# Two-batch attention and mixture-of-experts kernel: another order of the query groups (0 1 2 3 5 6 7 4), groups 0 and 4 in halves, keys of two groups loaded by heads where the batch changes

## The chip, the core and the metric

The kernel runs on one core of a Trainium2 chip. The metric is the device time of one execution in microseconds (us); the lower the better. TensorE is called PE in the rows, VectorE DVE, ScalarE ACT, GpSimd POOL, and the engine that issues all DMAs SP.

## What is computed

The input is x of shape (2, 2048, 256): two batches of 2048 tokens, that is 16 tiles of 128 tokens per batch, 32 tiles in all. Two blocks follow each other, and a layer norm stands behind each.

```python
x = layernorm(x + local_attention(x))          # windows of 128 queries, 256 keys
x = layernorm(x + ffn_block(x))

def ffn_block(x):                              # 16 heads of width 16, causal over 2048 keys
    q_in = k_in = rope(x)
    scores = einsum('bqhd,bkhd->bhqk', q, k) / sqrt(16)
    attn = softmax(where(causal, scores, -inf))
    attn_out = (attn @ v) @ out_proj_w.T + out_proj_b
    x1 = layer_norm(x + attn_out)
    gates = softmax(x1 @ gate_w.T + gate_b)    # 8 experts, the 2 best are kept
    moe_out = sum over the 2 best of gate * (x1 @ expert_w[e].T + expert_b[e])
    return layer_norm(x1 + moe_out)
```

## The kernel before

The work is cut into steps, and each step belongs to one engine.

**Early stage of a tile** (steps whose names begin with a and r, one set per tile of 128 tokens): the local attention, its layer norm, the rotary embedding, the projections to q, k and v, and the split of q and k into three bf16 parts, which are stored to DRAM. Key parts are loaded into `ks` (steps kst), query parts into `qs` (steps qst).

**Attention of a query group**: four tiles are one group of 512 queries. Groups 0 to 3 are batch 0, groups 4 to 7 batch 1. Group s of a batch sees the keys of the groups up to itself in the batch, so groups 3 and 7 see 16 key tiles, and groups 0 and 4 see 4. A group is worked off in jobs of four heads each. A job has three parts. First `mx`: scores with queries as rows (L1373, with a mask at L1377), whose row maxima VectorE takes (L1065). The negated maxima are split, transposed (L1382) and stored as three more rows of `qs` (L806). Then `st`: scores with keys as rows, with the maxima subtracted by those three rows (L1401, mask L1406), and ScalarE's exponential into `pbuf` (L978). Then `pv`: after each four key tiles one run of products with v (L1424, 32 instructions of the hardware). `mx` of the next job is interleaved with `st` of the present one. At a job's end ScalarE empties the sum (osb), PE transposes it (L1430), VectorE divides (L1109, L1119).

**Late stage of a tile** (steps d, f, g): transposition of the context (L1506), output projection (L1513), layer norm on VectorE and GpSimd (to L1210, which writes x1), transposition of x1 (L1518), gate product (L1523), the choice of two experts on VectorE (L1218 to L1274), transposition of the weights (L1527), bias product (L1532), four expert blocks f_e0 to f_e3 (L1537), sums on VectorE, ScalarE and GpSimd, two layer norms on VectorE (L1304 to L1334), the store. A tile's late stage needs all four heads' jobs of its tiles. Its buffers exist once for the tiles at places 0 to 28 in the order (`late_set` gives 0), so those go through it one behind another: the transposition of x1 of a tile waits for block f_e3 of the tile before (`("f_e3", l)`, and VectorE's g_y L1304 of the one before stands in front of parts of the next one's gate). Places 29, 30 and 31 have buffers of their own.

**Order.** `ORDER` lists the groups; a group in `HALVED` is worked off in two halves of two tiles, so in eight jobs instead of four. `plan()` puts all steps of all engines into one list: a greedy pass that takes the step that can begin first by the durations written in the code, and of those that begin together the one with the lowest rank. The rank of an early step is its tile number less 5 and some (`turn`). Each engine executes its steps in that order, whatever the chip's real times are. Group 4 (`s == GB`) is the first of batch 1; its keys go into the part of `ks` that group 0's keys held. They are loaded by heads (steps kh, L768): the keys for heads 0 to 3 once the last group of batch 0 is through with these heads, and so on; all other keys of batch 1 wait for the end of batch 0.

```python
ORDER = (0, 1, 2, 3, 4, 5, 6, 7)
HALVED = (0, 7)
LATE = [GT * s + u for s in ORDER for u in range(GT)]
add("d_x1T", T, "PE", 215, ("d_aff", T), ("f_e3", l))
add("f_acc0", T, "DVE", 330, ("f_b", T), ("d_aff", T), ("g_aff2", l))
add("f_wT", T, "PE", 100, ("f_ws", T), ("f_b", l), ("f_es", l))
```

Of the kernel before, what the change touches and what calls it, by code (L numbers as in the profile page):

```python
# [22 lines left out]
GT = 4  # L23
# [3 lines left out]
HJ = 4  # L27
# [20 lines left out]

ORDER = (0, 1, 2, 3, 4, 5, 6, 7)
HALVED = (0, 7)  # L50
LATE = [GT * s + u for s in ORDER for u in range(GT)]
JOBS = [(s, hg, j0, GT // (1 + (s in HALVED))) for s in ORDER for j0 in ((0, GT // 2) if s in HALVED else (0,))
        for hg in range(H // HJ)]
NJ = len(JOBS)


# [75 lines left out]
def pair_count(pair):  # L132

    return sum(1 for x in range(pair % 4, pair + 1, 4) if x * 2 // GT != GB)

# [57 lines left out]
def stage_steps():  # L193
# [3 lines left out]
    def add(name, T, engine, ns, *before):  # L197
        turn = {"a": -1.0, "d": 5.0, "f": 6.0, "g": 7.0, "w": -2.0}.get(name[0], 0.0) - (name[:4] == "load")
        if name[0] not in "dfg":
            turn -= 5  # L200
        rows[name, T] = engine, ns, T + turn + sum(x[0][0] == name[0] and x[1] == T for x in rows) / 32, \
            [x for x in before if x[1] >= 0]
# [19 lines left out]
    for T in range(NT):  # L222
# [36 lines left out]
        for k in range(3):  # L259
            s, L = T // GT, LATE.index(T)  # L260
            if s == GB:

                for hg in range(H // HJ):
                    add(f"kh{hg}{k}", T, "SP", 400, ("pst", T), ("pv_end", last_job(GB - 1) - H // HJ + 1 + hg))
            else:
                add(f"kst{k}", T, "SP", 400, ("pst", T), *[("ones_later", 0)] * (T >= LEAD),
                    *[("pv_end", last_job(GB - 1))] * (s > GB))
            add(f"qst{k}", L, "SP", 400, ("pst", T), *[("pv_end", last_job(L // GT - 2))] * (L >= 2 * GT))

    for T in range(NT):  # L270
# [35 lines left out]
        add("f_acc0", T, "DVE", 330, ("f_b", T), ("d_aff", T), ("g_aff2", l))  # L306
        add("f_e0", T, "PE", 1720, ("d_x1Tc", T))
        add("f_e0c", T, "DVE", 860, ("f_e0", T), ("f_acc0", T), ("f_wts", T))
# [26 lines left out]
def job_steps():  # L335
# [8 lines left out]
    for J in range(NJ):  # L344
# [6 lines left out]
        for i, (c, j, h, heads, cols) in enumerate(mx_list(J)):  # L351
            diag = c == s % GB
            rows["mx", J, i] = ("PE", heads * max(cols / 2.4 + 3, 98) + (220 if cols == P else 95 * heads) * diag, r + length * i / n,
                                [(f"kh{hg}{k}" if s == GB else f"kst{k}", newest) for k in range(3)] +
                                [(f"qst{k}", LATE.index(newest)) for k in range(3)])
            rows["mr", J, i] = ("DVE", heads * cols / 0.96 + 55, r + length * i / n,
                                [("mx", J, i)] + ([("nm_a", J - 1)] if J else []))
# [106 lines left out]
def build(nc, windows, cs, w_qk_t, w_out, in_t, in_b, wo_t, gate_t, exp_t, exp_b, rows, gate_b, out):  # L464
# [6 lines left out]
    with ExitStack() as ctx:  # L471
# [204 lines left out]
        def _(sp):  # L676
# [3 lines left out]
            for step in order:  # L680
# [67 lines left out]
                elif name[:3] == "kst":  # L748
                    s, pair = T // GT, T // 2
                    _, slot, n, a = STACKS[3 + int(name[3:])]  # L750
                    sp.wait_ge(parts_stored[e], 16 * early_count(T))
                    if s > GB:

# [7 lines left out]
                elif name[:2] == "kh":  # L761
# [5 lines left out]
                    r0 = T * (NPART * 2 * E) + (NPART + a) * E  # L767
                    sp.dma_start(ks5[slot * DH:(slot + n) * DH, GB % KRING, T % GT, hg * HJ:(hg + 1) * HJ],  # L768
                                 parts_dram[r0:r0 + n * E, :].rearrange("(d h) t -> d h t", h=H)[:, hg * HJ:(hg + 1) * HJ])\
# [568 lines left out]
        def _(pe):  # L1338
# [3 lines left out]
            for step in order:  # L1342
# [7 lines left out]
                if name == "mx":  # L1350
# [5 lines left out]
                    if i == 0 and hg == 0:  # L1356

                        for pair in range(k_known, (GT * s + j0 + nj) // 2):
                            if s != GB:
                                pe.wait_ge(k_loaded[pair % 4], PAIR * pair_count(pair))  # L1360
                        k_known = max(k_known, (GT * s + j0 + nj) // 2)
                        for pair in range((GT * pos + j0) // 2, (GT * pos + j0 + nj) // 2):
                            pe.wait_ge(q_loaded[pair % 4], PAIR * (pair // 4 + 1))
                    if i == 0 and s == GB:
                        pe.wait_ge(kh_loaded[hg], GT * 3 * 16)
                    kslot = ((s // GB) * GB + c) % KRING
# [222 lines left out]
```

## Time and profile before

| | |
|---|---|
| median of 3 runs | 1450.21 us (1449.8 to 1451.3) |
| the profiled execution's own time | 1447.28 us |
| its span, first to last instruction | 1445.5 us |
| PE busy | 1384.9 us, 96% |
| DVE busy | 1089.6 us, 75% |
| ACT busy | 783.6 us, 54% |
| POOL busy | 428.0 us, 30% |
| mean granted clock of PE | 0.993 of full speed |

Busy time is the union of an engine's instructions. A stretch less the PE time in it is what PE stood idle there. A busy PE counts the time in which a matmul is still under way while the next has begun, so a stretch with no idle time can still be slower than the matmuls alone would allow.

### The profile page before, as it was taken

The numbers are of one execution on the slowest core, as the hardware profiler recorded it, in microseconds if no ns is written. First come the engines' busy times: TensorE is split into PE (matmuls) and PEld (weight loads), VectorE is DVE, ScalarE is ACT, GpSimd is POOL, SyncE is SP. The second block draws the span as 40 slices with busy tenths as digits, with TensorE's granted clock in tenths as the row PEclk, the third lists the DMA queues.
The fourth block names the chain that finished last, engine by engine and source line by source line (L and its number), as shares of the span: only waits on it lengthen the run. The fifth ranks groups of instructions, "written<-read, shape, count | busy, mean of one in ns | idle before, by whom it ended". The sixth has DMA issues, their size and how long they took to land.

```text
span 1445.5 us, 28119 instructions
## 1 busy us (share of the span) xinstructions
PE 1384.9 (96%) x9600; PEld 773.2 (53%) x9600; DVE 1089.6 (75%) x2736; ACT 783.6 (54%) x1707; POOL 428.0 (30%) x707
## 2 busy tenths in 40 slices
PE   7899999999999999999999999999999999999995
PEld 6767655554455445354656655555443355555542
DVE  3765877887787887778655897888778787888745
ACT  3235365555665555666655445554656467665651
POOL 4434522322232231122343543333121110111233
PEclk9999999999999999999999999999999999999997
DMA  3865422230211121120116232222120011111100
GB/s 116 201 172 128 124 57 61 58 85 21 63 46 46 38 62 33 40 57 20 50 49 156 79 90 68 57 57 65 29 60 21 22 24 29 33 32 33 34 23 12
DMA packets 152560, 88.57 MB, mean 61 GB/s; under 512 B 114430, under 2 KB 145974, under 8 KB 152163
## 3 DMA queue, kind: packets, MB, share of 16 engines
q1 hardware_dynamic: 152419, 86.78, 23.2%
q8 instruction: 78, 1.28, 0.4%
q14 instruction: 63, 0.52, 0.1%
HBM read 60.71 MB, written 25.43 MB: 60 GB/s over the span
## 4 chain that ended last, share of the span: by engine, by line
PE 44%; DVE 4%; ACT 3%; issue 2%; SPq 2%; DMA 2%; POOL 1%; POOLq 0%; DVEq 0%; ACTq 0%
PE bank L1537 11%; PE bank L1424 10%; PE bank L1401 8%; PE bank L1373 7%; ACT pbuf L978 2%; DVE mxs L1065 2%; SPq L806 1%; DMA qs<-nmT 1%; PE bank L1494 1%; PE bank L1377 1%; PE bank L1406 1%; PE bank L1513 1%; PE bank L1472 1%; PE bank L1480 1%; PE bank L1523 1%
## 5 line engine op out<-in xcount | busy, mean ns | idle before, releaser
L1065 DVE TENSOR_REDUCE mxs<-bank 128x1 f32<-128x512 f32 (+3 forms) x1120 | 709.4, 667 | 150.1 <-PE bank L1373 79.6
L978 ACT ACTIVATE pbuf<-bank 128x512 f32<-128x512 f32 (+1 forms) x1112 | 588.6, 599 | 326.1 <-PE bank L1401 151.0
L1401 PE MATMUL bank<-qs,ks 99*128 99x256 bf16 (+3 forms) x1536 | 420.7, 319 | 16.4 <-DMA qs<-nmT 10.9
L1373 PE MATMUL bank<-ks,qs 96*128 96x512 bf16 (+3 forms) x1280 | 423.0, 349 | 4.9 <-DVE mxs L1065 2.5
L1424 PE MATMUL bank<-pbuf,vcur 128*17 128x256 f32 (+3 forms) x3072 | 253.5, 469 | 0.3
L1401 PEld LDWEIGHTS bank<-qs,ks 99*128 99x128 bf16 x1536 | 142.3, 98 | 172.1 <-issue 56.3
L1537 PE MATMUL bank<-ew,x1T 128*128 128x512 f32 x464 | 222.4, 601 | 0.4 <-DVE mxs L1065 0.3
L1373 PEld LDWEIGHTS bank<-ks,qs 96*128 96x128 bf16 x1280 | 123.3, 98 | 129.7 <-issue 40.6
L1424 PEld LDWEIGHTS bank<-pbuf,vcur 128*17 128x17 f32 x3072 | 79.8, 97 | 147.4 <-issue 109.6
L1537 PEld LDWEIGHTS bank<-ew,x1T 128*128 128x128 f32 x464 | 82.0, 190 | 72.3 <-issue 60.8
L958 ACT ACTIVATE etmp<-bank,small 128x256 f32<-128x256 f32 x116 | 48.7, 471 | 80.1 <-PE bank L1537 80.1
L1377 PE MATMUL bank<-maskb,idb 128*128 128x128 bf16 x384 | 81.4, 220 | 0.0
L927 POOL TENSOR_TENSOR accp<-accp,etmp 128x256 f32<-128x256 f32 x29 | 21.1, 727 | 201.1 <-ACT etmp L958 201.1
L923 POOL TENSOR_TENSOR accp<-etmp 128x256 f32<-128x256 f32 x29 | 21.1, 728 | 188.6 <-ACT etmp L958 188.6
L1406 PE MATMUL bank<-idb,maskb 128*128 128x128 bf16 x352 | 73.6, 220 | 0.0
L1296 DVE SCALAR_TENSOR_TENSOR acc<-bank,small,acc 128x256 f32<-128x256 f32 x58 | 27.9, 480 | 52.7 <-PE bank L1537 52.7
L1494 PE MATMUL bank<-rxT,inw 128*128 128x128 f32 x464 | 57.0, 276 | 0.0
L1494 PEld LDWEIGHTS bank<-rxT,inw 128*128 128x128 f32 x464 | 55.1, 192 | 2.2 <-issue 1.3
L899 POOL CAST parts<-qkf 128x512 bf16<-128x512 f32 x28 | 17.4, 623 | 122.9 <-DVE qkf L1159 122.9
L873 POOL TENSOR_SCALAR small<-small 128x1 f32<-128x1 f32 x32 | 7.1, 223 | 156.5 <-DVE small L1143 156.3
L1377 PEld LDWEIGHTS bank<-maskb,idb 128*128 128x128 bf16 x384 | 37.8, 98 | 13.7 <-issue 8.9
L958 ACT ACTIVATE osb<-bank 128x512 f32<-128x512 f32 (+1 forms) x40 | 20.5, 512 | 43.7 <-PE bank L1424 43.1
(279 smaller groups left out, 1746.2 us busy)
## 6 DMA issues: line engine op xcount, KB each, us to landing
vcur<-v_scratch SPq DMA_DIRECT2D x92, 136.0 KB, 2.3
parts_scratch<-parts SPq DMA_DIRECT2D x29, 384.0 KB, 3.3
xw<-windows SPq DMA_DIRECT2D x29, 256.0 KB, 2.8
qs<-parts_scratch SPq DMA_DIRECT2D x32, 192.0 KB, 3.3
ks<-parts_scratch SPq DMA_DIRECT2D x28, 192.0 KB, 3.4
qs<-parts_scratch SPq DMA_DIRECT2D x32, 128.0 KB, 3.1
v_scratch<-vst SPq DMA_DIRECT2D x29, 136.0 KB, 2.4
x_scratch<-x SPq DMA_DIRECT2D x29, 128.0 KB, 1.7
```

What stands on the lines that cost most here:

```text
L923: pool.tensor_tensor(accp[f], etmp[f][:, 0, :], etmp[f][:, 1, :], ALU.add).then_inc(accp1_ready, 1)
L958: return nc.scalar.activation(o, i, ACT.Copy, scale=scale)
L978: nc.scalar.activation(pbuf[:, u0:u0 + heads, nj * P - cols:nj * P], bk[:, 0:heads * cols].rearrange("p (h t) -> p h t", h=heads), ACT.Exp)\
L1065: v.reduce_max(mxs[:, j * HJ + h:j * HJ + h + heads, c], bk[:, 0:heads * cols].rearrange("p (h t) -> p h t", h=heads), AX_X)\
L1296: v.scalar_tensor_tensor(out=acc[f], in0=bk[:, 0:E], scalar=wts[f][:, 2 * k:2 * k + 1], in1=acc[f], op0=ALU.mult, op1=ALU.add).then_inc(ha ...
L1373: last = mm(bk[:, x * cols:(x + 1) * cols].rearrange("p (n t) -> p n t", t=P), qs5[0:KR, pos % QRING, j, head, :], ks5[0:KR, kslot, 0:cols ...
L1377: last = mm(bk[:, x * cols + j * P:x * cols + (j + 1) * P], idb[:, :], maskb[:, :], start=False, stop=True)
L1401: last = mm(bk[:, x * cols:(x + 1) * cols].rearrange("p (n t) -> p n t", t=P), ks5[0:KR + NPART, kslot, kb % GT, head, :], qs5[0:KR + NPAR ...
L1406: last = mm(bk[:, x * cols:x * cols + P], maskb[:, :], idb[:, :], start=False, stop=True)
L1424: last = mm(obank[32 * h:32 * h + DV, r0:r1], vcur[:, kb, h, :], pbuf[:, (u0 + h) % PB, r0:r1], start=kb == 0, stop=kb == nk - 1, tile_pos ...
L1494: last = mm(bk[:, co * P:(co + 1) * P], inw[:, ci, co * P:(co + 1) * P], rxT[e][:, ci, :], start=ci == 0, stop=ci == EC - 1)
L1537: last = mm(bk[:, :], x1T[f][:, c, :], ew[:, c, k * 2 * E:(k + 1) * 2 * E], start=c == 0, stop=c == EC - 1)
```

## The change

The order of the groups becomes 0 1 2 3 5 6 7 4. Group 7 is no longer worked off in halves, group 4 is, and it comes last. Group 5 now follows batch 0, so the keys of groups 4 and 5 (8 tiles) are loaded by heads. The ranks of early steps of tiles 16 to 31 become lower, so that they come earlier. Step f_e0 of a tile now also comes behind f_b of the tile before.

```diff
-ORDER = (0, 1, 2, 3, 4, 5, 6, 7)
-HALVED = (0, 7)
+ORDER = (0, 1, 2, 3, 5, 6, 7, 4)
+HALVED = (0, 4)
+AT_CHANGE = range(GB, ORDER[GB] + 1)
...
-    return sum(1 for x in range(pair % 4, pair + 1, 4) if x * 2 // GT != GB)
+    return sum(1 for x in range(pair % 4, pair + 1, 4) if x * 2 // GT not in AT_CHANGE)
...
         if name[0] not in "dfg":
-            turn -= 5
+            turn += -5 if T < 16 else -7 - (T - 16) / 4 if T < 24 else -9
...
-            if s == GB:
+            if s in AT_CHANGE:
                 for hg in range(H // HJ):
                     add(f"kh{hg}{k}", T, "SP", 400, ("pst", T), ("pv_end", last_job(GB - 1) - H // HJ + 1 + hg))
...
-        add("f_e0", T, "PE", 1720, ("d_x1Tc", T))
+        add("f_e0", T, "PE", 1720, ("d_x1Tc", T), ("f_b", T - 1))
...
-                    if i == 0 and s == GB:
-                        pe.wait_ge(kh_loaded[hg], GT * 3 * 16)
+                    if i == 0 and pos == GB:
+                        pe.wait_ge(kh_loaded[hg], len(AT_CHANGE) * GT * 3 * 16)
```

Line numbers of the changed kernel are one higher in these parts of the code. Nothing moves on PE before the first job of group 2 is half through. Behind that, these are places where the order differs.

PE in a job of group 7, around one run of products with v, first of before. `ks,qs` are `mx` scores, `qs,ks` are `st` scores, `pbuf,vcur` is the run.

```order
L1373 MATMUL bank<-ks,qs 128x512
L1401 MATMUL bank<-qs,ks 128x256 x2
L1373 MATMUL bank<-ks,qs 128x512
L1401 MATMUL bank<-qs,ks 128x256 x2
L1523 MATMUL bank<-gw,x1T 128x8 x2
L1424 MATMUL bank<-pbuf,vcur 17x256 x16
L1401 MATMUL bank<-qs,ks 128x256 x2
L1373 MATMUL bank<-ks,qs 128x512
L1401 MATMUL bank<-qs,ks 128x256 x2
L1373 MATMUL bank<-ks,qs 128x512
```

The same place in the changed kernel:

```order
L1374 MATMUL bank<-ks,qs 128x512
L1402 MATMUL bank<-qs,ks 128x512
L1374 MATMUL bank<-ks,qs 128x512
L1402 MATMUL bank<-qs,ks 128x512
L1538 MATMUL bank<-ew,x1T 128x512 x2
L1425 MATMUL bank<-pbuf,vcur 17x512 x16
L1374 MATMUL bank<-ks,qs 128x512
L1402 MATMUL bank<-qs,ks 128x512
L1374 MATMUL bank<-ks,qs 128x512
L1402 MATMUL bank<-qs,ks 128x512
L1374 MATMUL bank<-ks,qs 128x512
L1402 MATMUL bank<-qs,ks 128x512
```

What moved: the `st` scores come as one of 512 columns instead of two of 256, and the run of 16 products is 512 columns wide instead of 256.

PE at the end of the program, first of before: from the last run of products with v to the transposition of x1 of place 31.

```order
L1424 MATMUL bank<-pbuf,vcur 17x256 x12
L1424 MATMUL bank<-pbuf,vcur 17x128 x4
L1537 MATMUL bank<-ew,xT 128x512 x2
L1430 MATMUL bank<-idf,osb 128x128 x2
L1537 MATMUL bank<-ew,xT 128x512 x2
L1506 MATMUL bank<-idf,ctxn 128x128 x4
L1513 MATMUL bank<-wo,qs 128x256 x4
L1518 MATMUL bank<-idf,qs 128x128 x2
L1523 MATMUL bank<-gw,qs 128x8 x2
L1537 MATMUL bank<-ew,qs 128x512 x2
L1518 MATMUL bank<-idf,qs 128x128 x2
L1523 MATMUL bank<-gw,qs 128x8 x2
```

The changed kernel, behind its last run of products with v, in which tiles 26 to 31 (by place) are still in their late stage:

```order
L1519 MATMUL bank<-idf,x 128x128 x2
L1507 MATMUL bank<-idf,ctxn 128x128 x2
L1524 MATMUL bank<-gw,x1T 128x8 x2
L1538 MATMUL bank<-ew,x1T 128x512 x2
L1514 MATMUL bank<-wo,qs 128x256 x4
L1528 MATMUL bank<-idb,wpad 128x128
L1533 MATMUL bank<-ebp,accp 128x256
L1538 MATMUL bank<-ew,x1T 128x512 x6
L1519 MATMUL bank<-idf,x 128x128 x4
L1519 MATMUL bank<-idf,qs 128x128 x2
L1524 MATMUL bank<-gw,x1T 128x8 x2
L1538 MATMUL bank<-ew,x1T 128x512 x2
```

What moved: before, two expert blocks of the tile at place 29 and the whole late stage of places 30 and 31 stood behind the last run. Now three blocks of place 26 and most of the late stage of places 27 to 31 stand there, and of these 27 and 28 share one set of buffers with 26. The rows above begin with the transposition of x1 of place 27 and end with the gate product and the first block of place 28.

VectorE in the gate of a late tile near the end, from the gate's logits (L1218) on. First of before (tile at place 28):

```order
L1218 TENSOR_TENSOR small<-bank,gb_sb 128x8
L1304 TENSOR_TENSOR acc<-acc,etmp 128x256
L1221 TENSOR_REDUCE small<-small 128x1
L1307 BN_STATS small<-acc 128x6
L1312 BN_AGGR small<-small 128x2
L1224 RECIPROCAL small<-small 128x1
L1315 SCALAR_TENSOR_TENSOR acc<-acc,small,rowv 128x256
L1227 TENSOR_SCALAR small<-small 128x8
L1232 MAX small<-small 128x8
L1321 SCALAR_TENSOR_TENSOR x0f<-acc,small,x0f 128x256
L1235 MAX_INDEX ix<-small 128x8
L1325 BN_STATS small<-x0f 128x6
```

The changed kernel, in the gate of the tile at place 27, a few rows behind its first (L1219):

```order
L1233 MAX small<-small 128x8
L1316 SCALAR_TENSOR_TENSOR acc<-acc,small,rowv 128x256
L1236 MAX_INDEX ix<-small 128x8
L1189 TENSOR_TENSOR qs<-bank,qs 128x256
L1241 CAST small<-ix 128x8
L1322 SCALAR_TENSOR_TENSOR x0f<-acc,small,x0f 128x256
L1247 SCALAR_TENSOR_TENSOR small<-small 128x8 x2
L1192 BN_STATS small<-qs 128x6
L1326 BN_STATS small<-x0f 128x6
L1253 TENSOR_TENSOR small<-small 128x8
L1197 BN_AGGR small<-small 128x2
L1189 TENSOR_TENSOR qs<-bank,qs 128x256
```

What moved: between the same instructions of the gate now stand, besides those of the last layer norms of the tile before (L1316, L1322, L1326, L1331), those of the first layer norm of tiles 30 and 31 (L1189, L1192, L1197). From the logits to the padded weights (L1274, now L1275) it was 24 instructions, a row with x2 counted twice, and is 28 for the tile at place 27 and 33 for that at place 28.

## Rows read from the trace of the kernel before

**Rows 1.** The page: busy time of each engine, share of the span, instructions.

```profile
PE 1384.9 (96%) x9600; PEld 773.2 (53%) x9600; DVE 1089.6 (75%) x2736; ACT 783.6 (54%) x1707; POOL 428.0 (30%) x707
```

**Rows 2.** Windows: stretch, its length, busy time (instructions) of each engine, PE clock, DMA.

```profile
400.00:448.10 48.10, 47.14 (x308) 24.96 (x307) 37.76 (x91) 27.92 (x61) 13.97 (x22) 1.00 0.14 38
...
683.00:756.50 73.50, 72.09 (x486) 43.68 (x486) 44.41 (x126) 43.44 (x98) 28.26 (x45) 1.00 0.17 47
756.50:839.60 83.10, 80.84 (x565) 50.98 (x564) 58.22 (x176) 40.41 (x95) 36.84 (x61) 1.00 0.40 107
839.60:1043.10 203.50, 200.75 (x1313) 111.54 (x1310) 163.99 (x413) 109.35 (x242) 68.22 (x111) 1.00 0.24 64
...
1088.10:1133.00 44.90, 42.50 (x260) 17.16 (x258) 34.42 (x85) 26.36 (x57) 6.42 (x11) 1.00 0.08 20
1133.00:1178.90 45.90, 43.52 (x256) 17.97 (x256) 40.83 (x115) 26.09 (x56) 8.19 (x15) 1.00 0.09 24
1178.90:1268.70 89.80, 89.37 (x890) 50.01 (x888) 69.09 (x153) 62.18 (x127) 8.72 (x15) 1.00 0.13 30
1268.70:1361.90 93.20, 91.90 (x781) 50.27 (x779) 79.80 (x193) 57.42 (x121) 16.18 (x28) 1.00 0.14 34
1361.90:1400.90 39.00, 36.39 (x274) 19.85 (x273) 20.63 (x88) 23.19 (x55) 12.49 (x22) 1.00 0.10 29
1400.90:1435.00 34.10, 28.89 (x106) 13.37 (x105) 21.53 (x78) 7.88 (x24) 12.53 (x23) 0.90 0.03 9
```

**Rows 3.** Timeline around a 512-column run of products with v, group 6.

```profile
1106.48 3.63 PE L1424 MATMUL bank<-pbuf,vcur 128*17 128x512 f32 x32
...
1110.47 5.50 ACT L978 ACTIVATE pbuf<-bank 128x512 f32<-128x512 f32 x11 [2.21 <-PE bank L1401]
...
1110.69 1.89 DVE L1065 TENSOR_REDUCE mxs<-bank 128x1 f32<-128x512 f32 x3 [3.25 <-PE bank L1373]
```

**Rows 4.** Timeline around a 256-column run of products with v, group 7.

```profile
1289.36 1.92 PE L1424 MATMUL bank<-pbuf,vcur 128*17 128x256 f32 x32
...
1291.65 3.54 ACT L978 ACTIVATE pbuf<-bank 128x512 f32<-128x512 f32 x7 [0.93 <-PE bank L1401]
...
1291.86 4.61 DVE L1065 TENSOR_REDUCE mxs<-bank 128x1 f32<-128x512 f32 x8 [0.99 <-PE bank L1373]
```

**Rows 5.** Timeline of PE in the late stage of the tile at place 27.

```profile
1361.79 0.39 PE L1518 MATMUL bank<-idf,x 128*128 128x128 f32 x2
...
1370.81 0.22 PE L1527 MATMUL bank<-idb,wpad 128*128 128x128 bf16 x1 [0.56 <-DVE wpad L1274]
...
1371.80 0.27 PE L1532 MATMUL bank<-ebp,accp 128*128 128x256 bf16 x1 [0.33 <-ACT accp L958]
...
1378.18 1.88 PE L1537 MATMUL bank<-ew,x1T 128*128 128x512 f32 x4
...
1380.12 0.38 PE L1518 MATMUL bank<-idf,x 128*128 128x128 f32 x2
```

**Rows 6.** Timeline from the last run of products to the last tiles.

```profile
1402.60 1.71 PE L1424 MATMUL bank<-pbuf,vcur 128*17 128x256 f32 x32
...
1408.00 0.63 PE L1506 MATMUL bank<-idf,ctxn 128*128 128x128 f32 x4
...
1409.45 1.97 PE L1513 MATMUL bank<-wo,qs 128*128 128x256 f32 x8 [0.82 <-ACT qs L958]
...
1414.12 0.66 PE L1518 MATMUL bank<-idf,qs 128*128 128x128 f32 x2 [2.71 <-DVE qs L1210]
```

**Rows 7.** Timeline of VectorE in the gate of the tile at place 28.

```profile
1382.46 0.17 DVE L1218 TENSOR_TENSOR small<-bank,gb_sb 128x8 f32<-128x8 f32 x1 [3.30 <-PE bank L1523]
...
1387.84 0.17 DVE L1274 TENSOR_TENSOR wpad<-small,wpad 128x8 bf16<-128x8 f32 x1
```

**Rows 8.** Windows, same columns, a stretch with a lower granted clock.

```profile
1414.10:1420.60 6.50, 5.69 (x12) 2.77 (x12) 3.24 (x14) 0.96 (x4) 1.98 (x5) 0.51 0.07 23
```

**Rows 9.** SP's queue: first key loads by heads for the last four heads.

```profile
759.85 1.25 SPq L768 DMA_DIRECT2D ks<-parts_scratch  x3
```

More of the change, by code:

```diff
@@ L266, in stage_steps @@
                 add(f"kst{k}", T, "SP", 400, ("pst", T), *[("ones_later", 0)] * (T >= LEAD),
-                    *[("pv_end", last_job(GB - 1))] * (s > GB))
+                    *[("pv_end", last_job(GB - 1))] * (s >= GB))
             add(f"qst{k}", L, "SP", 400, ("pst", T), *[("pv_end", last_job(L // GT - 2))] * (L >= 2 * GT))
@@ L353, in job_steps @@
             rows["mx", J, i] = ("PE", heads * max(cols / 2.4 + 3, 98) + (220 if cols == P else 95 * heads) * diag, r + length * i / n,
-                                [(f"kh{hg}{k}" if s == GB else f"kst{k}", newest) for k in range(3)] +
+                                [(f"kh{hg}{k}" if s in AT_CHANGE else f"kst{k}", newest) for k in range(3)] +
                                 [(f"qst{k}", LATE.index(newest)) for k in range(3)])
@@ L751, in _ @@
                     sp.wait_ge(parts_stored[e], 16 * early_count(T))
-                    if s > GB:
+                    if s >= GB:
                         sp.wait_ge(pv_done, key_tiles_before(last_job(GB - 1) + 1))
@@ L767, in _ @@
                     r0 = T * (NPART * 2 * E) + (NPART + a) * E
-                    sp.dma_start(ks5[slot * DH:(slot + n) * DH, GB % KRING, T % GT, hg * HJ:(hg + 1) * HJ],
+                    sp.dma_start(ks5[slot * DH:(slot + n) * DH, T // GT % KRING, T % GT, hg * HJ:(hg + 1) * HJ],
                                  parts_dram[r0:r0 + n * E, :].rearrange("(d h) t -> d h t", h=H)[:, hg * HJ:(hg + 1) * HJ])\
@@ L1358, in _ @@
                         for pair in range(k_known, (GT * s + j0 + nj) // 2):
-                            if s != GB:
+                            if pair * 2 // GT not in AT_CHANGE:
                                 pe.wait_ge(k_loaded[pair % 4], PAIR * pair_count(pair))
```

## The prediction

> **What bounds the kernel now.** I read the page's busy times first: PE is busy 1384.9 of 1445.5 us, VectorE 1089.6 [rows 1]. So PE sets the time, and what the change is worth is what it adds to or takes from PE's work and PE's waits. Then I cut the span at the ends of jobs and read PE's idle time, length less PE time, from the windows [rows 2]. The reader is to see four kinds of stretch. With early stages beside the attention, PE stands idle 0.96 us in the 48.1 us of a group 2 job. Two jobs of group 6 without any early stage left have 2.40 and 2.38 us in 45. Group 7 in halves has 0.43 and 1.30 us in 183 us, also without early stages. The end, from the last job on, has 2.61 and 5.21 us. The change of batch (683.0 to 839.6) has 1.41 and 2.26 us, the 203.5 us behind it 2.75 us.
>
> The third thing read is why a whole job of group 6 waits more than a half job of group 7. Around a run of products with v of 512 columns, 3.63 us long, ScalarE's exponentials then start after 2.21 us of idleness and VectorE's maxima after 3.25 us [rows 3]. Around a run of 256 columns, 1.92 us long, these are 0.93 and 0.99 us [rows 4]. PE fills no bank for them during a run; a short run lets both nearly bridge it with the full banks at hand, a long one does not. VectorE is busy 34.42 us in the 44.9 us of such a job [rows 2], and what it loses in a run it must make up between runs, where it has little room.
>
> **The change, part by part.** The sum is made against the profiled execution's own 1447.28 us, 1.78 us more than its span. It stands 2.9 us below the median of the runs, 1450.21 us; I add the difference to the median at the end.
>
> *Group 7 whole.* Its work without halves is the same in columns. The cost is that its four jobs become like those of group 6 without early stages: the order has all early stages finished by then, as it has for those two jobs. A job of group 6 has three long runs and 2.4 us of idleness; one of group 7 has four, so at most 2.4 x 4/3 = 3.2 us, 12.8 us for four jobs. Taken off are the 1.73 us that the halves have [rows 2]: +11. The lower bound is the group 2 job, 0.96 us, which has stages to fill in: 3.8 - 1.7 = +2. I take the middle, **+6.5**, since each job of group 7 still has about one late stage to put behind its long runs.
>
> *Fewer runs.* Two runs of 256 columns take 3.84 us, one of 512 takes 3.63 [rows 3, 4], so 0.21 us is saved for each pair. Group 7 goes from 32 short runs to 16 long ones, -3.4 us; group 4 goes from 4 to 8, +0.8 us. Together **-2.6**. A score of 512 columns for two of 256 saves nothing by itself. If ScalarE's and VectorE's idleness cancels this, it is already in the line above.
>
> *The change of batch.* Group 4's four small jobs leave it. There PE is idle 3.67 us in 156.6 us [rows 2]; at the pace behind it, 2.75 us in 203.5 us, that would be 2.1 us, so -1.6 us. Early stages now run ahead through groups 2 and 3 and give them more to fill in with; group 2's 0.96 us per job shows how little is left there, some tenths. I take **-2**, with -3.7 (no idleness at all) and +3 as ends. The +3 is for the keys: three loads by heads take SP 1.25 us [rows 9], and the last four heads now need 24 of them, about 10 us of SP's queue, instead of 12. Behind them stand loads of x, the maxima rows and v. But the keys of these heads are needed only two jobs later, and the 203.5 us behind the change hold the four jobs of group 5 and one of group 6 [rows 2], so two jobs of group 5 are some 70 us, where before two small jobs of group 4 stood. So nothing is late, and I cost the doubled loads at nothing.
>
> *The end.* This is the largest and least certain part. The late stages of group 7 (places 24 to 27) now have only group 4's second half of attention beside them, and group 4's own four tiles come behind. Places 24 to 28 share one set of buffers, so they go one behind another: transposition of x1, gate, weights, four blocks, the next transposition. For the tile at place 27 this round took 1361.79 to 1380.12, 18.3 us, and PE was full in it but for 0.56 and 0.33 us [rows 5], because a half job of group 7 with its scores and runs filled it. What has to be waited for without such cover comes from two rows. From the end of a tile's last block (1378.18 + 1.88 = 1380.06) to the padded weights of the next (1387.84 + 0.17) it was 7.95 us; VectorE did 24 instructions from 1382.46 on, 0.23 us each [rows 5, 7]. In the changed order 28 stand there for place 27 and 33 for place 28, which gives 8.9 and 10.0 us. PE has for place 27 a block (1.88), the projections of two tiles (1.97, [rows 6]) and three small steps (0.39 each): 5.0 us, idle 3.9. For place 28 it has a block and eight small steps: 5.0 us, idle 5.0. Each time 0.75 us more between weights and bias product (0.99 us from 1370.81 to 1371.80 less the step itself; before, scores stood there). That makes 10.4 us. Places 25 and 26 have some 9 us to cover with a block, a projection, a run and scores, 7.4 us: 3 us for both. Place 24 starts the chain: from the end of the last run to the transposition of the context 1404.31 to 1408.00, then 0.82 us, then 1409.45 to 1414.12 for the first layer norm [rows 6]; before, blocks of an older tile filled the first of these, now scores and a run fill most: 5 us. Sum 18.4 us against the 7.8 us that stand there now: +10.6. Since I counted the covering scores roughly, and low, I take **+8**, with +3 and +18 as ends. The last four tiles are interleaved as the last two are now, and the 10.5 us behind the last block stay.
>
> Sum: 6.5 - 2.6 - 2 + 8 = +9.9 us, so 1457.2 us for a profiled execution, and **1460 us** for the median.
>
> Nothing else moves: PE's order is the same up to the middle of the first job of group 2, and f_e0's new condition only bites in the last three tiles.
>
> **A rule weighed against the trace.** The long run costs 3.63 us against twice 1.92 us, and leaves VectorE idle 3.25 us against 0.99 us [rows 3, 4]. The Trainium skill, Perfetto Trace Analysis, section Optimizing Tensor Performance, says that larger matmuls are more efficient than smaller ones where possible. By this rule alone group 7 whole would be a gain of 2.6 us with no cost, and the sum would be +3.4 us instead of +9.9.
>
> **Rivals.**
> *The end is covered after all (faster; 0.12).* Place: the late stages of places 24 to 28. If group 4's attention (scores and runs of eight short jobs; a run as in [rows 6] is 1.71 us) slides into the gaps, PE waits there little more than for the last tiles as now. It decides from 5 us of PE idleness in the last 110 us on: the end's term is then -3 or lower, and the sum is below -1.1; with group 7 at its lower end, +2, it is -5.6: 1445 us. For it: in group 7's halves late stages were covered almost entirely [rows 2]. Against it: the gate's chain is longer than PE's own work in a late stage, and behind the last run nothing but late stages is left.
> *No change (0.13).* Group 7 at +3 and the end at +2: 1450 us. For it: both are sums of waits that an interleaved order can hide.
> *The clock falls more than once at the end (0.15).* In the stretch 1414.10 to 1420.60, behind 2.71 us of idleness [rows 6], the granted clock was 0.51, and PE was busy 5.69 us of 6.5 [rows 8], 2.8 us of it lost. The changed end has two or three waits of that length. Two more such stretches give +6 to +7 on top of +9.9: 1467 us. The Trainium skill, TensorE: Matmul & The Clock Gate, section HAM oscillation, says that idle gaps in a stream of matmuls let the clock fall back to half; by it this case would be the likely one, and the one fall behind 2.71 us agrees.
> *The keys come late at the change (0.05, within the range).* PE would wait for a DMA of `ks` near 740 to 790 us: some +5.
> The forecast case has 0.55, with 1453 to 1467 us of its own.
>
> **How the numbers follow.** No change of less than 0.2%, 2.9 us, can be told from none here. Faster has the first rival, 0.12; within 0.2% the second, 0.13; slower the rest, 0.75. The range leaves out most of the first rival and the far end of the clock's: 1450 to 1470 us. All bounds together at one side would give 3 - 3.7 + 2 - 2.6 = -1 and 18 + 3 + 11 - 2.6 = +29; that many at once is unlikely.
>
> **What would show it.** Right: four jobs of group 7 near 2 to 3 us of PE idleness each; 15 us or more of PE idleness from group 7's last scores to the last block; PE waiting for `wpad` (L1275) twice for 3 to 5 us; less than 2.5 us idle around the change of batch. Wrong would be: PE idle below 10 us in the end; group 7's jobs at 1 us; a wait for `ks` from `parts_scratch`; or any part of groups 0 to 3 with a new wait of some length.

## The result, and the profile after

The changed kernel takes 1469.34 us, median of 4 runs (1468.99 to 1470.81), beside 1450.29 us for the kernel before in the same session: ratio 1.0137, 95% interval 1.0122 to 1.0151. That is 19.05 us slower; the prediction said 9.9 us slower. The profiled execution has 1469.29 us of its own, with a span of 1467.3 us, 21.8 us longer than before; the execution profiled before was 2.9 us below its median, so the spans differ by more than the medians. The page's busy times:

```profile
PE 1395.5 (95%) x9024; PEld 749.5 (51%) x9024; DVE 1093.5 (75%) x2736; ACT 783.8 (53%) x1707; POOL 426.8 (29%) x707
```

PE has 576 instructions fewer than in [rows 1], with the same columns in all, and is "busy" 10.6 us longer. About half of that is the clock: up to its last instruction PE ran 23.9 us at half clock, before 13.7 us, which is 5.1 us more lost. The rest is slower pace that counts as busy. The windows show where: the change of batch with group 5, group 7, group 4, the late stages behind it, what lies behind the last block, and two short stretches in group 7 (length, PE, PE's weight loads, VectorE, ScalarE, GpSimd, granted clock, DMA share, GB/s).

```profile
779.00:917.00 138.00, 136.97 (x906) 77.00 (x905) 105.42 (x261) 77.57 (x171) 48.54 (x79) 1.00 0.28 75
1105.00:1338.40 233.40, 222.96 (x1358) 92.59 (x1356) 184.69 (x446) 138.36 (x291) 28.82 (x52) 0.99 0.09 24
1338.40:1392.10 53.70, 49.41 (x440) 29.87 (x440) 26.51 (x104) 33.73 (x78) 15.78 (x28) 1.00 0.14 33
1392.10:1454.30 62.20, 54.57 (x188) 27.03 (x188) 43.70 (x163) 14.93 (x46) 28.21 (x49) 0.95 0.10 28
1454.30:1467.30 13.00, 0.00 (x0) 0.00 (x0) 6.89 (x17) 0.84 (x2) 5.10 (x10) 0.70 0.06 20
1121.50:1124.90 3.40, 3.40 (x8) 1.49 (x7) 2.51 (x10) 0.66 (x3) 0.79 (x2) 0.50 0.00 0
1295.60:1299.00 3.40, 3.40 (x17) 1.88 (x16) 1.91 (x5) 2.33 (x6) 0.00 (x0) 0.50 0.00 0
```

Group 7 has 10.4 us of PE idleness (233.40 less 222.96). Its halves had 1.73 us in 183 us for seven of the eight half jobs, and 2.6 us in the 39.0 us of the last one, which stood beside late stages [rows 2]. The last two rows are full PE work at half clock, 1.7 us lost in each.

Idle time alone does not show all of it. So I worked out the "column work" of each stretch of the program: what PE's instructions there take at their usual pace. A run of 512 columns counts 16 x 512 / 2400 = 3.41 us, and took 3.63 [rows 3]; every other instruction counts the distance, start to start, that its form usually has from the next one in these traces, as 0.219 us for a score of 512 columns (its columns alone, divided by 2.4 GHz, are 0.213) and 0.112 us for one of 256. "Lost" is the stretch's length less that work; it holds idleness, half clock and slow pace alike. The first stretch begins with PE's first instruction, 4.0 us after the start; a group's stretch ends with its last score with keys as rows; "behind the scores" goes on to the last block, and "behind the last block" to the last instruction.

| lost, us | groups 0 to 3 | change, 4 and 5 | 6 | 7 | group 4 at the end | behind the scores | behind the last block | column work |
|---|---|---|---|---|---|---|---|---|
| before | 66.4 | 11.8 | 18.6 | 17.0 | | 9.7 | 10.5 | 1307.3 |
| after | 69.4 | 5.4 | 19.2 | 30.2 | 7.2 | 12.6 | 13.0 | 1306.3 |
| group 7 in halves (e2) | 69.6 | 5.3 | 20.5 | 15.4 | 6.7 | 9.1 | 13.0 | 1307.6 |

By bare columns alone the work is 1262.5 us in both kernels, and group 7 goes from 24.2 to 36.0 us lost (22.5 in e2): the size depends a little on the measure, the order does not. Of groups 0 to 3, 2.3 us are in group 0, where both kernels have the same instructions in the same order; 1.7 of them are one more stretch at half clock. I count them as one execution's scatter. What is left: the change of batch gave 6.4 us, group 7 took 13.2 us, the end took 12.6 us. Before, the last half job of group 7 stood beside the late stages and lost 4.5 us of the 17.0; counted with the end, as the prediction counted it, group 7 goes from 12.5 (seven of eight half jobs) to 30.2 (the whole group) and the end from 24.7 to 32.8, +17.7 and +8.1 us.

What PE waits for in group 7 (first table, the changed kernel, 1105.0 to 1338.4) and in the late stages behind the last scores (second, 1392.1 to 1454.3); us in total, times, longest:

```profile
PE bank L1402 <- DMA qs<-nmT: 5.3, 4, 2.2
PE bank L1402 <- DVE mxs L1066: 1.2, 4, 0.3
PE bank L1519 <- DVE x L1211: 1.0, 1, 1.0
...
PE bank L1425 <- ACT pbuf L979: 0.2, 1, 0.2
```

```profile
PE bank L1528 <- DVE wpad L1275: 4.8, 2, 2.8
PE bank L1524 <- ACT x1T L959: 1.3, 2, 0.6
```

The four jobs of group 7 in the changed kernel, one by one:

```profile
1105.00:1170.40 65.40, 61.05 (x357) 24.90 (x355) 53.27 (x119) 35.30 (x73) 7.78 (x14) 0.97 0.16 42
1170.40:1227.30 56.90, 54.64 (x320) 21.35 (x320) 44.42 (x100) 34.82 (x71) 6.67 (x12) 1.00 0.08 18
1227.30:1285.40 58.10, 56.74 (x329) 22.67 (x328) 47.26 (x109) 35.45 (x73) 9.19 (x17) 1.00 0.08 22
1285.40:1338.40 53.00, 50.52 (x357) 23.67 (x355) 39.73 (x121) 32.79 (x74) 5.18 (x9) 0.97 0.04 11
```

PE is idle 4.35, 2.26, 1.36 and 2.48 us in them, and they lose 12.0, 6.5, 5.5 and 6.3 us.

Half of group 7's idleness is one wait per job: the first score with keys as rows (L1402) waits until the negated maxima, which three more rows of `qs` hold, have come back from their store. It took 1.89, 0.55, 0.58 and 2.23 us. The wait of the first job, with all that PE had ahead of it (timeline of PE; start, length, idle time ahead in brackets):

```profile
1119.30 0.41 PE L1519 MATMUL bank<-idf,x 128*128 128x128 f32 x2 [1.03 <-DVE x L1211]
...
1120.27 0.58 PE L1524 MATMUL bank<-gw,x1T 128*128 128x8 f32 x4 [0.35 <-ACT x1T L959]
1120.71 0.38 PE L1374 MATMUL bank<-ks,qs 96*128 96x512 bf16 x1
1120.93 3.05 PE L1538 MATMUL bank<-ew,x1T 128*128 128x512 f32 x4
1123.76 0.31 PE L1383 MATMUL bank<-idb,nmp 128*128 128x128 bf16 x1
...
1125.91 0.81 PE L1374 MATMUL bank<-ks,qs 96*128 96x512 bf16 x3
1128.61 0.38 PE L1402 MATMUL bank<-qs,ks 99*128 99x512 bf16 x1 [1.89 <-DMA qs<-nmT]
```

From the transposition of the maxima (L1383) to this score it is 4.85 us. Here PE has only maxima scores and late steps, with part of them at half clock; then it has nothing. In the other three jobs this way takes 4.8 to 5.1 us. The block of 3.05 us took 1.93 us elsewhere: it is the half clock.

The kernel before had the same wait, in its whole jobs. This is what PE waited for in the two jobs of group 6 without early stages, 1088.1 to 1178.9 in [rows 2], which were idle 2.40 and 2.38 us:

```profile
PE bank L1401 <- DMA qs<-nmT: 3.1, 2, 1.8
PE bank L1401 <- ACT pbuf L978: 0.4, 2, 0.2
```

So 3.1 of these 4.8 us, too, were the wait for the maxima rows, once per job, and not one that grows with the number of runs.

### The profile page after: what moved, and what is told of

Read it like the earlier page. It is cut to its first block, busy times and chain, and to the rows that moved or that the text cites. A ratio compares the mean times of both kernels' runs of the same rounds, so it can differ in the third digit from the quotient of the medians.

```text
span 1467.3 us, 26955 instructions
## 1 busy us (share of the span) xinstructions
PE 1395.5 (95%) x9024; PEld 749.5 (51%) x9024; DVE 1093.5 (75%) x2736; ACT 783.8 (53%) x1707; POOL 426.8 (29%) x707
## 4 chain that ended last, share of the span: by engine, by line
PE 36%; DVE 5%; ACT 3%; issue 3%; POOL 1%; SPq 1%; DMA 1%; POOLq 0%; DVEq 0%; ACTq 0%
PE bank L1425 9%; PE bank L1538 9%; PE bank L1402 6%; PE bank L1374 5%; ACT pbuf L979 3%; DVE mxs L1066 2%; SPq L807 1%; PE bank L1514 1%; DMA qs<-nmT 1%; PE bank L1378 1%; PE bank L1495 1%; PE bank L1407 1%; PE bank L1524 1%; PE bank L1473 0%; PE bank L1431 0%
## 5 line engine op out<-in xcount | busy, mean ns | idle before, releaser
L1402 PE MATMUL bank<-qs,ks 99*128 99x512 bf16 (+3 forms) x1344 | 421.2, 341 | 19.0 <-DMA qs<-nmT 12.5
L1425 PE MATMUL bank<-pbuf,vcur 128*17 128x512 f32 (+3 forms) x2688 | 250.9, 512 | 3.6 <-ACT pbuf L979 3.3
L1538 PE MATMUL bank<-ew,x1T 128*128 128x512 f32 x464 | 225.9, 610 | 0.2
L1402 PEld LDWEIGHTS bank<-qs,ks 99*128 99x128 bf16 x1344 | 127.2, 98 | 178.5 <-issue 53.7
L1425 PEld LDWEIGHTS bank<-pbuf,vcur 128*17 128x17 f32 x2688 | 69.8, 97 | 155.3 <-issue 129.3
L959 ACT ACTIVATE qT<-bank 128x256 f32<-128x256 f32 x59 | 22.7, 385 | 38.4 <-PE bank L1456 22.1
```

The source lines that it names most:

```text
L959: return nc.scalar.activation(o, i, ACT.Copy, scale=scale)
L1402: last = mm(bk[:, x * cols:(x + 1) * cols].rearrange("p (n t) -> p n t", t=P), ks5[0:KR + NPART, kslot, kb % GT, head, :], qs5[0:KR + NPAR ...
L1425: last = mm(obank[32 * h:32 * h + DV, r0:r1], vcur[:, kb, h, :], pbuf[:, (u0 + h) % PB, r0:r1], start=kb == 0, stop=kb == nk - 1, tile_pos ...
L1538: last = mm(bk[:, :], x1T[f][:, c, :], ew[:, c, k * 2 * E:(k + 1) * 2 * E], start=c == 0, stop=c == EC - 1)
```

## The experiments

Each kernel ran beside the kernel before, whose median was 1448.9 us (e1 to e4), 1450.9 (e5 to e8), 1448.5 (e9 to e11) and 1449.8 (e12).

**e1: group 7 whole in the old order.**

```diff
 # the kernel before
-HALVED = (0, 7)
+HALVED = (0,)
-add("f_e0", T, "PE", 1720, ("d_x1Tc", T))
+add("f_e0", T, "PE", 1720, ("d_x1Tc", T), ("f_b", T - 1))
```

> The kernel before in its old order 0 to 7, with group 7 whole (only group 0 in halves), and with the condition of the changed kernel that a tile's f_e0 stands behind the bias product of the tile before. Nothing is left out of the computation. Theory A (the whole jobs of group 7 are slower by themselves: 30.3 us beside the column work instead of 12.5 for the halves, since long runs of products starve ScalarE and VectorE): at least +15 us, and the last four tiles' late stages now all begin after the last job, some +5 more: 1465 to 1475 us. Theory B (group 7 whole is slow in the changed kernel only because of what stands beside it there, the end of group 6 before it and group 4 behind it, or because of the clock's two half stretches of 3.4 us): here it costs the forecast +6.5 or less, 1450 to 1458 us.

1474.54 us, ratio 1.0178 (1.0137 to 1.0219), +25.6 us. Group 7 and what follows up to the last block lost 52.3 us, before 26.7. So whole jobs cost at least as much without group 4 behind them: theory A. Two things swell the number. Of this stretch 17.1 us ran at half clock, before 6.8, so 5.1 us more were lost by that; and four tiles' expert blocks, not 2.7, stand behind the last scores. What the condition of f_e0 costs alone was not tried.

**e2: the changed kernel with group 7 in halves.**

```diff
 # the changed kernel
-HALVED = (0, 4)
+HALVED = (0, 4, 7)
 # o_den: the reciprocal waits for the division of the job before
+if T:
+    dve.wait_ge(*drain("o_T", T - 1))
```

> The changed kernel with group 7 in halves again (groups 0, 4 and 7 in halves), order 0 1 2 3 5 6 7 4 as it is. Nothing is left out. Theory A (whole jobs cost 17.8 us between group 7's first job and the last block, less 2.6 us that fewer runs save): 1469.3 - 15 = 1454 us, 1450 to 1458; PE's idle time in group 7 falls from 10.5 to about 2 us. Theory B (the place in the order costs, not the whole jobs): 1465 to 1470 us, and PE's idle time in group 7 stays near 10 us.

1450.75 us, ratio 1.0008 (0.9997 to 1.0018): 18.6 us of the changed kernel's time are gone, all but 1 or 2 us of what it had added: theory A. Windows of e2 (group 7, group 4, behind the scores):

```profile
1106.70:1327.40 220.70, 218.15 (x2000) 122.36 (x1999) 179.85 (x461) 141.63 (x299) 32.50 (x58) 1.00 0.15 36
1327.40:1384.90 57.50, 55.41 (x461) 31.97 (x460) 35.88 (x122) 32.65 (x75) 15.93 (x26) 0.97 0.15 38
1384.90:1438.30 53.40, 48.14 (x177) 23.81 (x174) 39.87 (x154) 14.26 (x44) 25.42 (x45) 0.97 0.07 23
```

and PE's longest waits in its group 7:

```profile
PE bank L1404 <- DVE mxs L1066: 0.9, 3, 0.4
PE bank L1385 <- DVE nmp L1098: 0.4, 1, 0.4
```

The wait for the maxima rows is gone. One of the eight half jobs, from the transposition of its maxima (L1385) to its first score with keys as rows (L1404), timeline of PE:

```profile
1232.46 0.22 PE L1385 MATMUL bank<-idb,nmp 128*128 128x128 bf16 x1
...
1232.97 1.88 PE L1540 MATMUL bank<-ew,x1T 128*128 128x512 f32 x4
1234.68 0.38 PE L1376 MATMUL bank<-ks,qs 96*128 96x512 bf16 x1
1234.90 1.88 PE L1540 MATMUL bank<-ew,x1T 128*128 128x512 f32 x4
1236.62 0.38 PE L1404 MATMUL bank<-qs,ks 99*128 99x256 bf16 x2
```

Here the way is 4.2 us and full of two expert blocks. In the eight half jobs it takes 3.3 to 13.4 us, each time without a wait of note at its end. So the rows are ready within 3.3 us in a half job at the least distance, where a whole job has them 4.8 to 5.1 us after the transposition. Group 7's loss falls by 14.8 us: 7.9 us of idleness (10.4 to 2.6), 3.4 us of the two half-clock stretches, and the rest, 3.5 us, of pace. The end loses 4.0 us less too: behind the last scores stand 80 instructions of the expert blocks instead of 92, five tiles' worth instead of 5.75. The spans differ by 16.0 us and not by 18.6, since the profiled execution of e2, 1453.24 us, was 2.5 us above its median, with a fall of the clock in group 6 (1024.9 to 1031.7, 3.4 us lost) that the changed kernel's trace does not have.

**e3: the new ranks in the old order.**

```diff
 # the changed kernel
-ORDER = (0, 1, 2, 3, 5, 6, 7, 4)
-HALVED = (0, 4)
+ORDER = (0, 1, 2, 3, 4, 5, 6, 7)
+HALVED = (0, 7)
```

> The changed kernel's code with the order 0 to 7 and groups 0 and 7 in halves: only the new ranks of the early steps and the new condition of f_e0 are left of the change. Theory A (the 6.3 us that the change of batch gained are from group 4's small jobs leaving it): 1450 us within 2 us. Theory B (they are from the early steps, which now run ahead through groups 2 and 3): 1444 to 1447 us.

1463.19 us, ratio 1.0088 (1.0068 to 1.0109). Both theories missed. Groups 5 and 6 of e3 against those of before:

```profile
872.40:1011.20 138.80, 134.49 (x844) 66.73 (x842) 111.30 (x290) 73.71 (x161) 35.82 (x60) 0.99 0.18 48
1011.20:1194.20 183.00, 172.08 (x1041) 73.51 (x1039) 150.78 (x375) 103.45 (x221) 26.08 (x49) 0.99 0.12 30
```

```profile
839.50:991.00 151.50, 150.28 (x991) 86.01 (x989) 122.95 (x315) 80.96 (x181) 55.70 (x90) 1.00 0.25 66
991.00:1178.80 187.80, 180.81 (x1113) 81.22 (x1111) 151.67 (x382) 106.71 (x228) 37.25 (x62) 1.00 0.15 39
```

PE idleness goes from 1.2 to 4.3 us in group 5 and from 7.0 to 10.9 in group 6; lost, from 25.1 to 37.4 us. The early steps were done four jobs sooner (in the second job of group 5 instead of the second of group 6), and whole jobs without them lose more, as in group 7. 3.4 of the 12.3 us are two stretches at half clock that the trace before does not have there. The condition of f_e0 is in e3 as well, so the ranks and the condition are priced together. The gain at the change of batch is not from the ranks: group 4 alone loses 5.4 us in e3 as well, 5.3 before. What is left as its cause is that group 4's small jobs leave that place.

**e4: runs of products over two key tiles, everywhere.** The ring of exponentials keeps its four.

```diff
 # the changed kernel
-VRUN = 4
-PB = VRUN * HJ
+VRUN = 2
+RING = 4
+PB = RING * HJ
 # ScalarE's wait on the ring: RING for VRUN
```

> The changed kernel with runs of products over two key tiles instead of four, everywhere; the buffer of exponentials still holds four key tiles. A run of 512 columns is then about 1.9 us instead of 3.6, there are twice as many. Nothing is left out. Theory A (the length of the run starves ScalarE and VectorE): group 7 gets back some two thirds of its 17.8 us, groups 5 and 6 a few us, against some 72 more switches at about 0.1 us each, 7 us: 1455 to 1463 us, and PE idle in group 7 below 5 us. Theory B (not the run's length, but the whole job's wider scores or the lack of early and late stages to fill in with): nothing comes back, only the switches cost: 1474 to 1480 us.

1469.94 us, ratio 1.0138 (1.0118 to 1.0158): no difference to the changed kernel. By parts it lost 6.0 us less in group 7 (24.2) and 3.2 and 3.6 us more in groups 6 and 5. But all four runs of e4 have a lower granted clock (0.983 to 0.985; the changed kernel's 0.986 to 0.989), and its trace has 41.0 us at half clock up to PE's last instruction, where the changed kernel's has 23.9: 8.6 us more lost. In group 6 alone 10.2 us ran at half clock, 5.1 us lost, more than the 3.2. So shorter runs saved something that the clock took back. Neither theory as it stood; e9 has short runs in group 7 alone.

**e5: order 0 1 2 3 5 6 4 7.**

```diff
 # the changed kernel
-ORDER = (0, 1, 2, 3, 5, 6, 7, 4)
-HALVED = (0, 4)
+ORDER = (0, 1, 2, 3, 5, 6, 4, 7)
+HALVED = (0, 7)
```

> The changed kernel with the order 0 1 2 3 5 6 4 7 and groups 0 and 7 in halves: group 4 stands whole between groups 6 and 7, group 7 ends the kernel in halves as before. Nothing is left out. Theory A (the change of batch without group 4's small jobs gains 6.3 us, group 7 in halves and an end with large jobs cost what they cost before): 1449 - 6 = 1443 us, 1441 to 1446. Theory B (early and late stages that stood beside other groups are missing somewhere, as in the old order with the new ranks, 1463 us): 1450 us or more, with the loss in the jobs of group 6 and 4.

1455.18 us, ratio 1.0046 (1.0031 to 1.0062): theory A missed, and theory B had the time but not the place. The change and group 5 lost 5.5 us, as hoped, but group 7 22.7 and the scores' end 12.1 (before 17.0 and 9.7): group 4's short jobs took fewer late steps with them, and these came back in group 7 and the end: 7.75 tiles' expert blocks stood beside group 7, where the kernel before had 6.1. The gain at the change was given back.

**e6 and e8: group 6, and groups 5 and 6, in halves in the kernel before.**

```diff
 # the kernel before
-HALVED = (0, 7)
+HALVED = (0, 6, 7)      # e6
+HALVED = (0, 5, 6, 7)   # e8, with e2's wait in o_den
```

> The kernel before with group 6 in halves too (groups 0, 6 and 7). Theory A (a whole job without early stages beside it loses about twice what its two halves lose): the three jobs of group 6 that have none lose 14.3 us now and would lose 7 to 9: 1443 us, 1441 to 1446. Theory B (the halves gain in group 7 only): 1448 to 1453 us.

> The kernel before with groups 5 and 6 in halves too (groups 0, 5, 6 and 7); a further wait that costs nothing orders VectorE's reciprocal of a job behind the division of the job before. Theory A: group 5's whole jobs have early stages beside them and lose only 1.4 to 2.0 us each, so halving them brings nothing and costs some 2 us for more runs: 1443 to 1447 us, no better than group 6 alone. Theory B (halving is good everywhere): 1438 to 1442 us.

e6: 1449.73 us, ratio 0.9994 (0.9984 to 1.0004), in the range of theory B. e8: 1451.02 us, ratio 1.0005 (0.9994 to 1.0015), above both ranges. In e6 group 6 lost 12.8 us instead of 18.6, as theory A has it, and yet no time is gained: group 7 lost 21.4 instead of 17.0, behind the scores 13.0 instead of 9.7, and 1.0 us of column work is more. The 3.3 us behind the scores match the clock's part: 13.7 us at half clock there, before 6.8. Group 5 in halves lost 6.7 us instead of 6.5: halving brings nothing where early stages stand beside.

**e7: the changed kernel with the old ranks.**

```diff
 # the changed kernel, early steps
-turn += -5 if T < 16 else -7 - (T - 16) / 4 if T < 24 else -9
+turn -= 5
```

> The changed kernel with the old ranks of the early steps (tile number less 5), all else as in it. Theory A (the new ranks only move early steps to where they are needed, and what they cost in the old order, 14 us, is that groups 5 and 6 run out of them two jobs sooner; here the new order uses them up at the same job as before): without them group 5's first job would wait for its keys: 1472 to 1480 us. Theory B (the ranks cost here too): 1457 to 1465 us.

1503.25 us, ratio 1.0374 (1.0352 to 1.0396). The order needs its ranks, by more than either theory said, and at other places: group 6 lost some 16 us more than in the changed kernel, group 7 some 10 (23.9 of its 239.9 us at half clock), group 5 some 7 and group 3 some 5. The longest piece is ahead of group 6's first score with keys as rows, where PE did early and late steps and maxima scores for 76.5 us and stood idle 10.1 us.

```profile
905.00:981.50 76.50, 66.42 (x355) 42.93 (x353) 64.23 (x179) 17.90 (x49) 38.03 (x62) 0.96 0.33 86
```

**e9: runs of two key tiles in group 7 alone.**

```diff
 # the changed kernel
+def run_of(J):
+    return 2 if JOBS[J][0] == 7 else VRUN
 # run_of(J) for VRUN wherever a run begins or ends
```

> The changed kernel with runs of products over two key tiles in group 7 alone; elsewhere four. Nothing is left out. With runs of two everywhere the last three jobs of group 7 lost 12.4 us beside their column work instead of 18.2, the first one 11.9 instead of 12.1, and the rest of the kernel gave this back. Theory A (the run's length is a third of group 7's cost; the first job's wait for its maxima and the scores of 512 columns are the rest): 1469.3 - 6 = 1463 us, 1461 to 1466. Theory B (what short runs gain in group 7 is given back in group 4 and the end, which are near their own limits): 1468 to 1471 us.

1464.59 us, ratio 1.0119 (1.0097 to 1.0140); the interval overlaps that of the changed kernel. The trace shows more: the profiled execution is below its median, the span 6.0 us shorter, and group 7 lost 24.0 us instead of 30.2. 1.7 of these 6.2 us are a half-clock stretch that did not come (one at 1122.6, none near 1295), 2.9 us are idleness (10.4 to 7.5). Its first rows of waits:

```profile
PE bank L1407 <- DMA qs<-nmT: 3.0, 3, 1.7
PE bank L1524 <- DVE x L1216: 1.0, 1, 1.0
```

So the length of the run is at most some 6 of the 14.8 us between whole jobs and halves, by one trace, 4.5 without that stretch. The other 9 to 10 go with the whole jobs themselves, their maxima rows ahead; no run divides these further.

**e10, e11, e12: which groups in halves, in the new order.**

```diff
 # the changed kernel, each with e2's wait in o_den
-HALVED = (0, 4)
+HALVED = (0, 7)         # e10
+HALVED = (0, 4, 6, 7)   # e11
+HALVED = (0, 6, 7)      # e12
```

> The changed kernel with group 4 whole and group 7 in halves (groups 0 and 7 in halves), order 0 1 2 3 5 6 7 4. Nothing is left out. Theory A (the end's cost is the late stages that stand behind the last scores with nothing to cover them; whole, group 4 lets none of its four tiles begin before its last job): the end loses 3 to 6 us more than with group 4 in halves, 1454 to 1457 us against 1450.75. Theory B (all late stages go one behind another anyway, so it does not matter how group 4 is cut): 1449 to 1452 us.

> The changed kernel with groups 0, 4, 6 and 7 in halves. Nothing is left out. Theory A (what halves save in group 6, 5.7 us, is given back behind it in group 7 and the end, 3.9 and 4.0 us, as with the old order): 1449 to 1453 us, like groups 0, 4 and 7 in halves. Theory B (the giving back belongs to the old order's end, whose late stages stood beside large jobs): 1443 to 1447 us, the fastest of all.

> The changed kernel with groups 0, 6 and 7 in halves and group 4 whole at the end, order 0 1 2 3 5 6 7 4: the two cuts that came out best put together. Nothing is left out. Theory A (halving group 6 is worth some 3 us in this order, as between groups 0, 4, 7 and groups 0, 4, 6, 7 in halves, and group 4 whole some 1 us): 1444 to 1447 us beside 1448.5 for the kernel before, the fastest of all. Theory B (both only move the same late stages forward and do not add up): 1447 to 1449 us.

e10: 1448.75 us, ratio 1.0001 (0.9990 to 1.0011). Theory B, a quarter of a us below its range: group 4 and the scores' end lost 17.1 us and 11.4 us lay behind the last block, together 28.5; in halves it was 15.8 + 13.0 = 28.8. How group 4 is cut does not matter here. That it is because its tiles go through the late stages one behind another anyway is argued: of its four tiles only the one at place 28 shares the older tiles' buffers. e11: 1447.03 us, ratio 0.9988 (0.9979 to 0.9997), at the upper edge of theory B's range; e12, theory A: 1446.41 us, ratio 0.9975 (0.9966 to 0.9985), 3.4 us faster than the kernel before by the medians and the fastest of all. In this order halving group 6 pays. By the traces of e12 and e10 group 6 loses 5.4 us less and group 7 2.8 us more, and the stretch behind the scores does not grow (9.1 us lost in e11 as in e2; 11.3 in e12, 12.4 in e10, where 3.4 us more ran at half clock). So half of the gain is given back here too, and the other half stays. Groups 6 and 7, then group 4 and behind the scores, of e12:

```profile
915.40:1093.00 177.60, 175.57 (x1560) 101.54 (x1558) 145.35 (x367) 107.58 (x229) 36.11 (x63) 1.00 0.20 50
1093.00:1319.70 226.70, 223.09 (x2018) 124.51 (x2016) 190.77 (x475) 141.54 (x297) 31.02 (x53) 1.00 0.14 34
1319.70:1376.10 56.40, 54.30 (x385) 29.20 (x381) 37.24 (x121) 31.57 (x75) 18.54 (x32) 1.00 0.13 37
1376.10:1432.80 56.70, 49.37 (x178) 24.12 (x178) 41.64 (x157) 14.81 (x44) 26.83 (x47) 0.97 0.07 22
```

PE is idle 2.0 us in group 6 and 3.6 in group 7, where the changed kernel had 7.0 and 10.4.

## Why the prediction was right or wrong, step by step

The direction and the range held; the size was half of what was measured. 1469.34 us is 0.7 us inside the range and outside the forecast case's own 1453 to 1467 us, so it was in part luck that the range held.

- **Group 7 whole, +6.5, and fewer runs, -2.6.** This is the step that failed. Forecast +3.9 together, measured 17.7 us by the traces with the prediction's own bookkeeping (12.5 to 30.2), 13.2 us group 7 against group 7, 18.6 us by undoing it (e2), of which 4 are in the end. The idle time itself came out near: 10.4 us, 2.6 a job, inside the 2 to 3 named. That is luck of the mean, since the jobs had 4.35, 2.26, 1.36 and 2.48. But the term was made of idle time alone. The trace had more: two half-clock stretches (3.4 us), 3.5 us of slower pace inside "busy", and the late stages that whole jobs push behind them (4 us). Its upper bound, +11, was too low for the same reason. The mechanism was also only partly right. The prediction gave the idleness to long runs that starve ScalarE and VectorE and scaled group 6's 2.4 us a job by the number of runs, 4/3. Of those 4.8 us in two jobs, 3.1 were the wait for the maxima rows by DMA at the job's start, once per job; the trace before shows it, the rows around a run [rows 3] do not. In halves it is gone (5.3 us to none of note). For the long runs e9 shows 6 us at most. Middle between bounds was a poor choice: group 6's two jobs without early stages [rows 2] were the nearest row, and a group's first job without them was not among them.
- **The change of batch, -2.** Right sign, too small: -6.4 us for it with group 5. The prediction counted the idleness in 156.6 us (3.67 us); lost were 11.8 us from 756 to 991. The doubled loads of keys by heads cost nothing that the trace shows: 1.03 us of idleness in the 138 us from 779 on. The rival of the late keys did not come.
- **The end, +8.** As forecast in size, 8.1 us, not in its parts, so the size is luck. PE waited for `wpad` 2.84 and 1.91 us, not twice 3 to 5, and was idle 4.3 + 7.6 = 11.9 us from group 7's last scores on, not 15 or more. "The 10.5 us behind the last block stay" was wrong: 13.0. And 4 of the 8 us belong to group 7 whole, since e2 has 28.8 us there instead of 32.8.
- **Nothing else moves.** True for groups 0 to 3 in sum but for 0.7 us: with the early steps moved into it group 2 lost some 2.6 us more, and group 3 some 2 less. e3 shows that the same ranks, with the condition of f_e0, cost 14 us in the old order, where they empty groups 5 and 6 of early steps.
- **The clock rival.** At the end the two stretches at half clock were 3.4 us each, as much as the one of 6.8 us before: no loss there. So the rival's sign came and its price did not. But two new ones came in group 7, after 1.03 and 0.35 us of idleness at 1118 to 1120 and after 2.2 us at 1293. The Trainium skill, TensorE: Matmul & The Clock Gate, section HAM oscillation, says that idle gaps let the clock fall. These two falls came behind idle gaps, but the gap of 1.89 us at 1126.7 was followed by full clock (1.00 from 1128.6 to 1135.0): the length of one gap alone does not tell here whether the clock falls.
- **The rule on larger matmuls.** By the Trainium skill, Perfetto Trace Analysis, section Optimizing Tensor Performance, the sum would have been +3.4 us. The rows agree with it for the instructions themselves: in halves the whole program has 1.3 us more column work (1307.6 against 1306.3). It does not carry over to the time: what stood around the larger scores and runs of a whole group 7 cost 18.6 us.

**What is shown and what is argued.** That group 7 whole is the whole of the net loss is shown (e1, e2). That early steps beside whole jobs cover them is supported by e3, and by whole group 5 in the changed kernel, idle 1.03 us in 138 us with early steps beside it. That run length has a part in it rests on e9's trace; its times alone don't settle it. That a half job's maxima are ready in time is read from the traces; no kernel changed that alone, so how the loss divides between this wait and the wider jobs stays open. The falls of the clock differ too: up to PE's last instruction from 10.2 us at half clock in the trace of e12 to 41.0 in that of e4 and 54.6 in that of e7, and no run holds them fixed.

## What to carry to other kernels

Price a restructured loop by its elapsed time less its column work, not by the engine's idle time: here idle time showed 7.9 of 14.8 us. Cut work into more, smaller jobs where each begins with a round trip (maxima, store, reload) and nothing else is left to fill in with; where independent work stands beside, the cut brings nothing (group 5 in e8). Read what ended the waits in the row that a forecast is scaled from: it says what the row scales with. A gain in one stretch counts only when the stretches behind it are read as well: in e5 and e6 it was given back further on, in e12 half of the same cut was kept.

## What the runs showed of the hardware

Half-clock stretches of 3.4 us come as well as those of 6.8 us (and of 10.2 us, in e3, e4, e6 and e7), and they come in the middle of dense work: at 1121.5 and 1295.6 us PE was busy all of the 3.4 us at a granted clock of 0.50. An expert block's row of four instructions that takes 1.93 us elsewhere took 3.05 us there, and the row shows no idle time for it.
